# Macaron block with a state-space scan: sums of squares in four column tiles, roots sent from ACT, halves of the reciprocals, and orders of five queues

## The reference

```python
x = x + 0.5 * ffn(layernorm(x))
x = x + attn(layernorm(x))
x = x + 0.5 * ffn(layernorm(x))
```

```python
Bm = rmsnorm((x @ WB.T).reshape(B, L, H, N), Bn_w) + B_bias
Cm = rmsnorm((x @ WC.T).reshape(B, L, H, N), Cn_w) + C_bias
dt = softplus(x @ Wdt.T)
theta_cumsum = cumsum((x @ Wth.T).reshape(B, L, H, N // 2) * dt[..., None], axis=1)
Bm, Cm = rope(Bm, theta_cumsum), rope(Cm, theta_cumsum)
h_t = alpha_t * h_{t-1} + beta_t * (B_{t-1} x_{t-1}) + gamma_t * (B_t x_t)
y_t = C_t h_t
```

## Time and profile before

| | |
|---|---|
| median of 3 runs | 3594.47 us (3583.92 to 3598.4) |
| profiled execution, its time | 3601.3 us |
| its span, first to last instruction | 3599.5 us |
| PE busy | 2897.9 us (81%) |
| PE weight loads busy | 2199.6 us (61%) |
| DVE busy | 2374.4 us (66%) |
| ACT busy | 1820.9 us (51%) |
| POOL busy | 1539.4 us (43%) |
| mean granted PE clock | 0.882 of full |

### The profile page before, as it was taken

The page is one execution under the profiler, slowest core; times in us unless marked ns, Lnnn a source line. Parts: engine busy times, 40 slices in busy tenths (PEclk is TensorE's granted clock), DMA queues, the critical chain, the costliest instruction groups (busy, mean ns, idle before and its releaser), DMA issues.

```text
span 3599.5 us, 84310 instructions
## 1 busy us (share of the span) xinstructions
PE 2897.9 (81%) x28752; PEld 2199.6 (61%) x28752; DVE 2374.4 (66%) x3926; ACT 1820.9 (51%) x3740; POOL 1539.4 (43%) x1420
## 2 busy tenths in 40 slices
PE   5139957788888899999977999999899998279573
PEld 4128846466666657667654667676676676168462
DVE  5214224699999849889945988884888885243135
ACT  1016624566666356666614666663666672046331
POOL 3550050255555416655610555551455553510345
PEclk7559968889899899999978999998999998589785
DMA  9537755466665246556403666642666653467564
GB/s 387 197 123 254 255 163 179 142 183 184 177 184 176 77 139 171 164 162 171 134 3 119 173 172 172 171 134 68 170 172 171 172 160 115 158 206 254 175 205 138
DMA packets 311258, 605.54 MB, mean 168 GB/s; under 512 B 59136, under 2 KB 159616, under 8 KB 310016
## 3 DMA queue, kind: packets, MB, share of 16 engines
q1 hardware_dynamic: 286464, 535.63, 48.9%
q0 software_dynamic: 24576, 67.14, 5.6%
HBM read 446.25 MB, written 155.32 MB: 167 GB/s over the span
## 4 chain that ended last, share of the span: by engine, by line
PE 53%; DVE 19%; issue 10%; another core or an unknown queue 7%; ACT 4%; DMA 4%; POOL 1%; DVEq 1%; SPq 1%; POOLq 0%; ACTq 0%
PE bank L63 15%; PE bank L568 7%; PE bank L1327 4%; DVE tmp L1275 3%; PE bank L1197 3%; PE bank L1393 3%; DVE xbc L1251 3%; DMA rc_in<-decay_t 3%; PE bank L581 2%; PE bank L559 2%; PE bank L1391 2%; PE cs_sn L581 2%; PE bank L1367 2%; DVE rot L1275 2%
## 5 line engine op out<-in xcount | busy, mean ns | idle before, releaser
L63 PE MATMUL bank<-xh,wb 128*128 128x512 f32 x2048 | 685.4, 416 | 73.1 <-ACT btr L1342 43.2
L644 DVE TENSOR_TENSOR hh<-sg,bank 128x96 f32<-128x96 f32 x384 | 97.5, 254 | 596.4 <-ACT sg L619 372.6
L63 PEld LDWEIGHTS bank<-xh,wb 128*128 128x128 f32 x2048 | 373.3, 192 | 190.4 <-ACT btr L1342 63.9
L1206 ACT ACTIVATE xbc<-bank,norm_w 128x512 f32<-128x512 f32 x512 | 350.7, 685 | 240.8 <-PE bank L63 234.1
L1295 POOL TENSOR_TENSOR sq<-cst,rho 128x512 f32<-128x512 f32 x128 | 133.5, 1043 | 742.8 <-DVE xbc L1251 411.3
L1283 POOL TENSOR_TENSOR rot<-rot,tmp 128x512 f32<-128x512 f32 x256 | 341.8, 1335 | 238.3 <-DVE tmp L1275 238.3
L568 PE MATMUL bank<-wgu,xgT 128*128 (+1 forms) x1536 | 343.7, 350 | 107.6 <-issue 68.2
L63 PE MATMUL bank<-xl,wb 128*128 128x512 f32 x1024 | 408.5, 399 | 0.0
L1284 POOL TENSOR_TENSOR rot<-rot,tmp 128x512 f32<-128x512 f32 x256 | 358.7, 1401 | 0.0
L568 PEld LDWEIGHTS bank<-wgu,xgT 128*128 128x128 f32 x1536 | 261.0, 204 | 118.5 <-issue 118.1
L1275 DVE SCALAR_TENSOR_TENSOR rot<-xbc,bias,cs_sn 128x1024 f32<-128x1024 f32 x256 | 325.4, 1271 | 8.4 <-DVE xbc L1251 6.8
(11 more groups left out here) (277 smaller groups left out, 6084.7 us busy)
## 6 DMA issues: line engine op xcount, KB each, us to landing
wb<-watt_dram SPq DMA_DIRECT2D x96, 1024.0 KB, 7.7
rr_bc<-rr_dram SPq DMA_DIRECT2D x128, 512.0 KB
yd<-ys SPq DMA_DIRECT2D x96, 512.0 KB
wd<-w_down SPq DMA_DIRECT2D x384, 96.0 KB
watt_dram<-wb SPq DMA_DIRECT2D x32, 1024.0 KB, 5.4
dt_bc<-row_dram SPq DMA_DIRECT2D x256, 128.0 KB
al_bc<-row_dram SPq DMA_DIRECT2D x256, 128.0 KB, 3.2
xd<-xg SPq DMA_DIRECT2D x12, 2048.0 KB, 23.7
```

Source lines behind the costliest of these rows:

```text
L63: ins = e.matmul(dst, a, m, start=start and c == 0, stop=stop and c == n - 1, skip_group_check=not (start and stop))
L1206: e.activation(xbc[j % 4][:, i, :], of(i)[:, :], ACT.Copy, scale=norm_w[:, i:i + 1])
```

## The change

It has five parts.

1. Sums of squares: 512 tokens are split in two halves; B and C of the first half go to rows 0 and 32 of SSB, of the second to rows 64 and 96, as 128 x 32 tiles with 256 columns. There are eight matmuls a turn in place of four. The root reads 100 rows by 256, into a tile of its own.
2. The root comes ahead of T_act2 on ACT, and the rows to `rc_in` are sent from ACT's queue, behind T_act2, in two transfers of 64 partitions. The reciprocals still leave in one transfer; they lie by token halves in DRAM (16 rows of 256) and in `rr_bc`, which is loaded in pieces of 1 KB where it had 2 KB.
3. PE does the first transposes ahead of G, and they wait only for POOL's first half of rot (a new signal, e_Rb).
4. In scan 0 ACT splits high halves behind all four parts of A, and DVE takes the low halves behind F_dve2, in the following turn.
5. In scan 0 SP issues stores and load of the split weights behind the dt and end loads.

```diff
-        rr_bc = [sb(f"rr_bc{i}", [P, 4, SEQ]) for i in range(2)]
+        rr_bc = [sb(f"rr_bc{i}", [P, 2, 4, SEQ // 2]) for i in range(2)]
-        stdr = decay_t[0:36, :, :, :].rearrange("p k q a -> p (k q a)")
-        NORM_ROWS = slice(28, 36)
+        HALF = SEQ // 2
+        stdr = sb("stdr", [100, HALF])[:, :]
+        NORM_ROWS = [slice(28, 36), slice(92, 100)]
...
             A_act(e, b * NP + 1, 1, [2, 3])
             R_act(e, b * (NP // 2))
+            R_rows_act(e, b * (NP // 2))
...
             for eo in range(2):
-                for ty in range(2):
-                    first = 30 - 28 * (1 - ty) - 2 * (j % 2)
-                    ins = e.matmul(SSB[32 * ty:32 * ty + 32, :], one_hot[:, first:first + 32], sq4[:, 2 * ty + eo, :],
-                                   start=j % 2 == 0 and eo == 0, stop=j % 2 == 1 and eo == 1, skip_group_check=True)
+                for half in range(2):
+                    for ty in range(2):
+                        first = 30 - 28 * (1 - ty) - 2 * (j % 2)
+                        g = 64 * half + 32 * ty
+                        ins = e.matmul(SSB[g:g + 32, 0:HALF], one_hot[:, first:first + 32], sq4[:, 2 * ty + eo, half * HALF:(half + 1) * HALF],
+                                       start=j % 2 == 0 and eo == 0, stop=j % 2 == 1 and eo == 1, skip_group_check=True)
...
-            e.activation(stdr, SSB[0:36, :], ACT.Sqrt, scale=1.0 / NS, bias=eps_nm[0:36, 0:1]).then_inc(e_sr.sem, 1)
+            e.activation(stdr, SSB[0:100, 0:HALF], ACT.Sqrt, scale=1.0 / NS, bias=eps_nm[0:100, 0:1]).then_inc(e_sr.sem, 1)
...
-        def R_sp1(e, gm):
+        def R_rows_act(e, gm):
             e.wait_ge(e_sr.sem, e_sr.at(gm + 1))
             e.nop(nofuse=True)
             e.wait_ge(e_rc.sem, e_rc.at(gm))
             e.nop(nofuse=True)
-            e.dma_start(rc_in[:, :], stdr[NORM_ROWS, :].rearrange("r (c w) -> r c w", w=32)).then_inc(a_r1.sem, 16)
+            for h in range(2):
+                e.dma_start(rc_in[CL * h:CL * h + CL, :], stdr[NORM_ROWS[h], :].rearrange("r (c w) -> r c w", w=32)).then_inc(a_r1.sem, 16)
...
-                e.dma_start(rr_bc[par][CL * a:CL * a + CL, :, :], src.to_broadcast([CL, 4, SEQ])).then_inc(a_rr[par].sem, 16)
+                e.dma_start(rr_bc[par][CL * a:CL * a + CL, :, :, :].rearrange("p h g t -> p (h g) t"), src.to_broadcast([CL, 8, HALF])).then_inc(a_rr[par].sem, 16)
...
-                r = rr_bc[par][:, 2 * ty + j % 2, :]
-                both = xbc[j][:, 2 * ty:2 * ty + 2, :]
-                e.tensor_tensor(both, both, r.unsqueeze(1).to_broadcast([P, 2, SEQ]), ALU.mult).then_inc(dst.sem, 1)
+                r = rr_bc[par][:, :, 2 * ty + j % 2, :]
+                both = xbc[j][:, 2 * ty:2 * ty + 2, :].rearrange("p e (h t) -> p e h t", h=2)
+                e.tensor_tensor(both, both, r.unsqueeze(1).to_broadcast([P, 2, 2, HALF]), ALU.mult).then_inc(dst.sem, 1)
...
+                if ty == 0:
+                    ins.then_inc(e_Rb.sem, 1)
...
         def tr_pe(e, p, j, eo, x):
             if eo == 0:
-                e.wait_ge(e_R.sem, e_R.at(p + 1))
+                e.wait_ge(e_Rb.sem, e_Rb.at(p + 1))
...
                 if K:
+                    tr_pe(e, p, jp, 0, 0)
                     G_pe(e, p, jp)
-                    tr_pe(e, p, jp, 0, 0)
...
                     T_act3(e, n, j)
+                if RG:
+                    R_act(e, gm + 1)
                 if T:
                     T_act2(e, n + 1, j + 1)
                 if RG:
-                    R_act(e, gm + 1)
+                    R_rows_act(e, gm + 1)
...
+                if A:
+                    A_act(e, n + 3, j + 3, [2, 3], behind_transposes)
                 if is_first(b) and not last:
                     wb_high_act(e, q + 4, j, it * 2 + j // 2 + 2)
                 if is_first(b) and not (last and j >= 1):
                     th_high_act(e, q + 3, j + 1, it * 2 + (j + 1) // 2 + 1)
-                if A:
-                    A_act(e, n + 3, j + 3, [2, 3], behind_transposes)
...
                 F_dve2(e, n, j, b * (NP // 2) + it * 2 + j // 2 + 1)
+                if is_first(b) and not (first and j == 0) and not (last and j >= 1):
+                    wb_low_dve(e, q + 3, j + 1)
+                if is_first(b) and not (first and j == 0) and not (last and j >= 2):
+                    th_low_dve(e, q + 2, j)
                 if T:
                     T_dve2(e, n + 1, j + 1)
...
-                if is_first(b) and not last:
-                    wb_low_dve(e, q + 4, j)
-                if is_first(b) and not (last and j >= 1):
-                    th_low_dve(e, q + 3, j + 1)
```

More of the change, by code:

```diff
@@ L212, in build @@
         row_dram = nc.dram_tensor("row_dram", [NP, 2, ROWW], F32, kind="Internal").ap()
-        rr_dram = [nc.dram_tensor(f"rr_dram{i}", [8, SEQ], F32, kind="Internal").ap() for i in range(2)]
+        rr_dram = [nc.dram_tensor(f"rr_dram{i}", [16, SEQ // 2], F32, kind="Internal").ap() for i in range(2)]
         a_const, a_x = arr("a_const"), arr("a_x")
@@ L1109, in prep_sp @@
                     e.dma_start(dst.rearrange("q (t c) -> q t c", t=TT), s4[:, :, kp, :]).then_inc(a_roww.sem, 16)
-            R_sp1(e, b * (NP // 2))
             e.wait_ge(a_roww.sem, a_roww.at(8 * (b + 1)))
@@ L1211, in R_act @@
             e.wait_ge(e_ssm.sem, e_ssm.at(2 * (gm + 1)))
-            e.wait_ge(a_r1.sem, a_r1.at(gm))
-            e.activation(stdr, SSB[0:36, :], ACT.Sqrt, scale=1.0 / NS, bias=eps_nm[0:36, 0:1]).then_inc(e_sr.sem, 1)
+            e.wait_ge(a_r1.sem, a_r1.at(2 * gm))
+            e.activation(stdr, SSB[0:100, 0:HALF], ACT.Sqrt, scale=1.0 / NS, bias=eps_nm[0:100, 0:1]).then_inc(e_sr.sem, 1)
         def R_dve(e, gm):
-            e.wait_ge(a_r1.sem, a_r1.at(gm + 1))
+            e.wait_ge(a_r1.sem, a_r1.at(2 * (gm + 1)))
             e.wait_ge(a_r2.sem, a_r2.at(gm))
@@ L1288, in build @@
         e_own, e_Dp = ev("e_own"), ev("e_Dp")
+        e_Rb = ev("e_Rb")
         def own_pool(e, n, q):
@@ L1550, in turn_sp @@
                 gm = b * (NP // 2) + it * 2 + j // 2
-                if is_first(b) and not (last and j >= 1):
-                    wb_store_sp(e, q + 3, j + 1)
-                if is_first(b) and not last:
-                    wb_load_sp(e, b, q + 4, j)
-                if is_first(b) and not (last and j >= 2):
-                    th_store_sp(e, q + 2, j)
                 if not (last and j >= 2):
@@ L1563, in turn_sp @@
                     end_sp(e, q + 2, j + 2)
+                if is_first(b) and not (last and j >= 1):
+                    wb_store_sp(e, q + 3, j + 1)
+                if is_first(b) and not last:
+                    wb_load_sp(e, b, q + 4, j)
+                if is_first(b) and not (last and j >= 2):
+                    th_store_sp(e, q + 2, j)
                 if not (last and j >= 1):
@@ L1572, in turn_sp @@
                         wb_load_sp(e, b, q + 4, j)
-                if RG:
-                    R_sp1(e, gm + 1)
                 if not (last and j >= 2):
@@ L1593, in pairs_pe @@
             Y_pe(e, p - 1, j - 1, (b + 1) * (NP // 2) - 1)
+            tr_pe(e, p, j, 0, 0)
             G_pe(e, p, j)
-            tr_pe(e, p, j, 0, 0)
             z_pe(e, b, 2)
```

## The result

The changed kernel took 3615.62 us, the median of 13 runs (3604.78 to 3635.62); the kernel before, beside it, 3599.89 us (3583.92 to 3606.43). The ratio is 1.0053, with a 95% interval of 1.004 to 1.0066: slower by half a per cent, where 3450 us was forecast. The profiled execution took 3623.18 us (span 3621.4), at a mean granted clock of 0.860 where before had 0.882.

A forecast was written before the change was run, and what follows sets the result against it. DVE bounds scan 0; PE and DVE both near their limit in scans 1 to 3. Gains of 76 (scans 2 and 3), 39 (scan 1) and 30 us (scan 0), together 145, bring 3594.5 to 3450; range 3405 to 3530.

The forecast's parts named there:

- Root and rows: Odd turns: root ahead of T_act2, rows from ACT leave 0.9 to 1.2 us earlier; DVE's wait, 0.98 a pair, goes.
- PE's clock: Scans 1 to 3: granted clock stays about 1.0; at 0.91 PE's 26.7 a pair would be 29.3, most gain lost.
- Squares in four tiles: PE's squares, every turn: eight 256-column matmuls on four tiles, group from 1.91 to about 1.05 us, gain 0.86 a turn.
- rivals A: Squares on PE: column tiles run only two at a time; 108 us gained, 3486 us; chance 0.15.
- D: Squares on PE: smaller records follow without overlap, taking twice 1.91 us; kernel slower, 3675 us; chance 0.03.
- PE below DVE's floor, and the gain above it free: Scans 1 to 3: PE alone needs 26.7 a pair, under DVE's 27.2, so DVE becomes the bound.
- DVE's wait for G going wholly: Scan 2: DVE's wait for G, 13.1 us over 26 turns, goes wholly once DVE is behind PE.
- The charge of 0.3 a pair for ACT's new order: ACT, odd turns: late L1162 and two DMA issues together cost 0.3 us a pair, bounds 0 and 1.0.
- Scan 0: Scan 0 on DVE: one of two low halves freed from GpSimd's blocking, 1.08 us a turn, 28 turns, 30 us.
- rival C: Scan 0: both of DVE's low halves are freed, 31 us more gained, 3419 us; chance 0.12.
- Rival B: Odd turns wait for ACT, its late L1162 and both issues costing 1 us more a pair: 3495 us; chance 0.13.

The follow-up runs named there:

- e8: Kernel before with the change's scan 0 orders, and the rows sent from ACT in one transfer right behind the root: 3331.1 us, ratio 0.9924.
- e6: Kernel before with one edit: in odd turns of scans 1 to 3 SP issues the next wb load behind the rows: 3313.25 us, ratio 0.9858.
- e2: Changed kernel with the squares of before (four 512-column matmuls, two column tiles), rows in one transfer from ACT, layouts of before: 3366.54 us, ratio 1.0057.
- e1: Changed kernel with one edit: in odd turns of scans 1 to 3 SP issues the wb load behind the rows: 3276.42 us, ratio 0.9791.
- e4: Changed kernel with four unread 512-column matmuls a turn added on PE behind the squares: 3334.18 us, ratio 0.9958.
- e7: Changed kernel with squares in two tiles as before, rows in one transfer from ACT, and SP's wb load behind the rows: 3272.14 us, ratio 0.974.
- e3: Kernel before with only the change's scan 0 orders on ACT, DVE and SP: 3351.16 us, ratio 1.0003.

## Why the prediction was wrong

The step that failed is the one on the rows' way, under "Root and rows". It gave the way two bounds, "the same 5.68 plus the second issue, or some 2 us less", and concluded that the wait goes at either end, because the rows leave earlier. Both bounds took the way as a length that starts at the issue. It isn't one: with the 1 MB load issued 1.7 to 2.8 us ahead, the rows land about when that load is through (they are used 8.51, 8.94 and 9.10 us after its issue, in before, after and e8). Leaving earlier then only makes the way longer, and the wait of DVE, forecast at nothing, went from 0.98 a pair to 19.5/12 = 1.6. The number was in the earlier trace rows: a load issued 2.83 us ahead, seen and set aside because the new queue is empty. e6 shows it from the other side: with only the order of the load turned, the kernel before gains 1.4%. How the load holds the rows up inside the DMA engines is not shown.

The second term that failed was put at nothing: PE's clock, taken to stay at 1.0. PE, shortened, waited for H (20.6 us in 390 of scan 2, before 2.3) and its clock fell to 0.93. The late rows account for the gain that didn't come; that the kernel became slower than before took the clock as well.

The page "DMA: Bandwidth & Descriptors" of the Trainium skill says, under Queues, rings and completion order, that an engine takes turns between queue rows packet by packet. No run here shows a small transfer on ACT's queue getting past the load in that way: 7.28 (after) and 6.46 us (e8) from issue to use with the load ahead, against 4.00 at most in e6 with the load behind. What its Rules for kernel authors say, that two transfers to disjoint halves don't run faster than one, agrees with e2: 6.83 with one, 7.53 with two.

Point by point:

- **Squares in four tiles**: right in size. 1.07 us against the forecast 1.05; rivals A and D fell.
- **PE below DVE's floor, and the gain above it free**: the floor was right, 27.2 + 0.3 = 27.5 forecast and 27.95 in e1, with DVE at 95% as named. In after it was never reached. PE, now ahead, idled at Y and its clock fell to 0.93; the prediction priced such a fall ("29.3", still under the 30.06 of before) as what would lose most of the gain, but gave it no chance of its own. It is worth some 35 us (e4).
- **DVE's wait for G going wholly**: wrong in after, 20.6 us, because G ran behind the wait at Y and on the lowered clock; right in e1, 3.3 us in 300.
- **The charge of 0.3 a pair for ACT's new order**: nfr waits 6.0/12 = 0.5 in after and 5.6/12 in e7, but close to nothing in e1 (0.5 us in 300); the size was about right where the wait arises.
- **Scan 0**: 39 us against the forecast 30. One low half freed (1218 ns instead of 2295), the other still blocked (1496), as reasoned: rival C fell. The working was incomplete, though: e3 shows that the orders alone give nothing, since the stores on SP then hold back the rows. The prediction passed over this, "behind them wait al and th loads, used a turn later: nothing". It would have been wrong if the rows had stayed on SP.
- **Rival B**, ACT late, 3495: ACT is not what the odd turn waits for (0.5 a pair).

None of the rivals ended slower by this mechanism: the one slow rival was about the tiles' overlap. The forecast of the state itself, DVE as the bound at 27.5 a pair, was right once the load was out of the way, but only in scans 2 and 3; e1's scan 1 took 30.34, where 28.5 was forecast.

## What to carry to other kernels

Ask of a small transfer on the path not only which queue it is on, but which large transfer was issued in the microseconds ahead of it on any queue; put the large one behind, and its way drops by more than an earlier issue could give. Before making PE shorter, see which engine will hold it up then: an idle gap that opens on PE can cost its clock, and the next group on the path runs at the lower level. When an instruction is moved on one engine, follow the stores and loads that wait for it on SP, and what stands behind these.
